# GpSimd writes a buffer of its own behind each gather, and waits for it once per pair

## The chip, the cores and the metric

One core of one Trainium2 chip runs the kernel. The metric is the device time of the whole launch in microseconds (us); here it is the median of several executions. The engines are called PE (TensorE), DVE (VectorE), ACT (ScalarE), POOL (GpSimd) and SP (SyncE). The trace also splits off PEld, the weight loads of TensorE.

## The reference, cut to what matters

A graph of 12,500 nodes with 128 features and 212,500 edges, sorted by their target node, goes through three rounds of message passing. Two use one of eight weight matrices per edge type, the third is a plain graph convolution.

```python
def _rgcn_layer(x, W, SW, b, src, dst, rel):          # twice, W is [8, 128, 128]
    xt = jnp.einsum('nd,rde->rne', x, W)
    msg = xt[rel, src]
    agg = jax.ops.segment_sum(msg, dst, num_segments=x.shape[0])
    return jax.nn.relu(agg + x @ SW + b)
...
x = _layernorm(x + _L0_gnn_ref(...))                   # two layers of the above
feat = jax.nn.relu(x @ W1 + b1)
h = feat * d_invsqrt
agg = jax.ops.segment_sum(h[src], dst, num_segments=N)
feat = feat - agg * d_invsqrt
x = _layernorm(x + feat @ W2 + b2)
```

## The kernel before, in words

**Tiles, groups, pairs, iterations.** The edges are cut into tiles of 128. Seven tiles (`KG`) are a group, two groups a pair (`PAIR`, so `PT` = 14 tiles), four pairs an iteration (`UN` = 56 tiles). A pass over the edges has 29 full iterations and a rest of three pairs, 119 pairs in all (`NGP`). There are three passes: r1 reads the input `x`, r2 reads `x1_d` (the result of r1, `x_d` in the trace), r3 reads `h_d`. r1 and r2 come from `relational_sum`, r3 from `plain_sum`, and all three get their rows from `Gathers`.

**The gathers.** For each tile POOL issues one indirect DMA (line 781) that fetches the 128 rows of the tile's source nodes into one of the 56 slots of `c.rows`. The indices lie in `c.idx`, which ACT copies into place one pair at a time (`take`, `put`, line 735). Each gather adds 16 to the semaphore `landed` of its group as its data arrives. Ahead of a pair POOL waits for two things: `idx_ready` (the indices are there) and `summed` (PE has finished the pair that stood in the same 14 slots one iteration, that is 56 tiles, earlier). So POOL can be at most four pairs ahead of PE. The first 14 tiles of r2 and 21 of r3 are fetched by `early` (line 761) while the pass before still ends.

**What takes the rows.** PE waits for a group's `landed`, multiplies each tile with a one-hot matrix `S` that DVE builds (line 1023 in r1 and r2, line 1216 in r3), and adds into a PSUM bank (line 961 in r1 and r2, line 1186 in r3); its last matmul of a group (in r3 of a pair) adds 1 to `summed`. In r1 and r2 ACT then copies the bank to `agg` (line 885), and once an iteration PE multiplies `agg` with the eight weight matrices (line 931) and DVE adds the outcome to `acc` (line 1062). In r3 DVE adds the bank to `acc` itself (line 1243). DVE's `one_hot` for the pair after next waits for `summed` of this pair. The node-wise work of a finished chunk (`Tail1` to `Tail3`, transposes such as line 1343) is placed between the pairs.

**Order.** Nothing schedules at run time: each engine runs its own instruction stream in the order of the code, and the streams meet at semaphores alone. POOL's stream in the passes is nothing but gathers, register arithmetic and the waits at a pair's start. `gate` adds 1 to a semaphore that nobody waits for.

Of the kernel before, what the change touches and what calls it, by code (L numbers as in the profile page):

```python
# [12 lines left out]
P = 128  # L13
# [12 lines left out]
PR = RING // PAIR  # L26
PT = PAIR * KG
# [10 lines left out]
class Part:  # L38


    def __init__(self, at, tiles):
        self.at, self.tiles, self.groups = at, tiles, len(tiles)
        self.pairs = range(at, at + len(tiles) // PAIR)
# [9 lines left out]
NGP = NG // PAIR  # L53
# [53 lines left out]
def gate(eng, passed):  # L107

    eng.sem_inc(passed, 1)
# [7 lines left out]
def build(nc, x, src, dst, rel, w1, sl1, b1, w2, sl2, b2, gw1, gb1, gw2, gb2, out):  # L117
    with ExitStack() as top:
        def sb(name, shape, dt=F32):
            return top.enter_context(nc.sbuf_tensor(name, shape, dt))  # L120
# [9 lines left out]
        c = Shared()  # L130
# [20 lines left out]
        c.gs_i = sb("gs_i", [1, RING + NG], I32)  # L151
        c.gs8 = sb("gs8", [1, NG])
        c.step_t, c.step_g, c.carry = sb("step_t", [P, 1]), sb("step_g", [P, 1]), sb("carry", [P, 1])
        c.found = sb("found", [NODES, DEG_COLS + COLS])
        c.deg = sb("deg", [DEG_ROWS, DEG_PARTS, NODES])
        c.dinv = sb("dinv", [P, NB])
# [524 lines left out]
def rounds_of(eng, c, which, most):  # L681
    return eng.value_load(c.rounds_i[0:1, which:which + 1], min_val=1, max_val=most)


def halves(part, h):


    tiles = part.of(h)
    return (tiles + 1) // 2 if part is not FULL and h >= (ENDS - 1) * PAIR else tiles


class Gathers:
# [3 lines left out]
    def __init__(self, nc, top, c, tag, table, which, turns, incs, then):  # L696
        def sem(name):
            return top.enter_context(nc.semaphore(f"{tag}_{name}"))

        self.c, self.table, self.which, self.incs = c, table, which, incs  # L700
        self.most = N // GN + 2 if which else 4 * (N // GN + 1) + 1
        self.turns, self.then = turns, then
        self.landed = [sem(f"landed{h}") for h in range(RING + PAIR)]
        assert [s.num - self.landed[0].num for s in self.landed] == list(range(RING + PAIR))
        self.cleared = sem("cleared")
        self.idx_ready = sem("idx_ready")
        self.summed = sem("summed")

# [57 lines left out]
    def run(self, pool, ready, stored):  # L766

        def iteration(q, i, part, set_of, skip=0):
            at = set_of * UN
            for p in part.pairs:  # L770
                if (p + 1) * PT <= skip:
                    continue
                pool.wait_ge(self.idx_ready, (q * (IT + 1) + i) * PR + p + 1)
                pool.wait_ge(self.summed, self.pairs_summed(q, i, p))
                gate(pool, self.c.passed)
                for h in range(p * PAIR, (p + 1) * PAIR):
                    for k in range(part.of(h)):
                        s, slot = h * KG + k, h if k < halves(part, h) else RING + h % PAIR
                        if s < skip:
                            continue  # L780
                        pool.indirect_dma_start(  # L781
                            out=self.c.rows[:, self.place(s), :], out_offset=None, in_=self.table[:, :],
                            in_offset=bass.IndirectOffsetOnAxis(ap=self.c.idx[:, at + s:at + s + 1], axis=0)
                        ).then_inc(self.landed[slot], 16)

        def one_round(q, skip=0):
            iteration(q, 0, FULL, 0, skip)
            with pool.Fori(0, IT // SETS) as n:
                i = pool.snap(n * SETS)
                iteration(q, i + 1, FULL, 1)  # L790
                iteration(q, i + 2, FULL, 0)
            iteration(q, IT, LEFT, 1)

        self.begin(pool)
        pool.sem_inc(self.cleared, 1)
        one_round(0, EARLY[self.turns])
        if ready is not None:
            pool.wait_ge(ready, 1)
            gate(pool, self.c.passed)
        rounds = rounds_of(pool, self.c, self.which, self.most)  # L800
        with pool.If(rounds > 1):
            with pool.Fori(1, rounds) as q:
                pool.wait_ge(self.summed, q * (self.incs * NGP) + self.incs * PR)
                gate(pool, self.c.passed)

                landed = range(self.landed[0].num, self.landed[0].num + len(self.landed))
                pool.dma_reset(landed)
                pool.sem_clear(landed)
                pool.sem_inc(self.cleared, 1)
                one_round(q)  # L810
        pool.end_ifs()
        if self.then is not None:
            self.early(pool, rounds, stored)

# [539 lines left out]
class Sets:  # L1354
# [14 lines left out]
    def sb(self, name, shape):  # L1369
        return self.ctx.enter_context(self.nc.sbuf_tensor(f"{self.tag}_{name}", shape, F32))  # L1370

    def sem(self, name):
        return self.c.top.enter_context(self.nc.semaphore(f"{self.tag}_{name}"))
# [413 lines left out]
```

## Time and profile before

| | before |
|---|---|
| time, median of 3 runs | 7520.16 us (7511.46 to 7523.07) |
| the profiled execution | 7492.37 us, of which the span of the core is 7490.5 us |
| POOL busy | 4709.2 us (63%), 4992 instructions |
| PE busy | 3400.0 us (45%) |
| DVE, ACT busy | 1713.6 us (23%), 399.8 us (5%) |
| DMA | 382.84 MB, 51 GB/s over the span |
| gathers of line 781 | 1661 in r1, 1647 in r2, 1640 in r3, together 4948 |

The profile lists for each instruction when it started and how long it was busy, and for each idle stretch ahead of one what ended it. "issue" is idle time that ended by nothing the profile can name, "remote" or "an unknown queue" one that ended by a semaphore whose sender the profile could not name. Busy shares are means over the whole span.

### The profile page before, as it was taken

To read this page: it belongs to the slowest core of one execution; us is meant where nothing else is said; L and a number is where in the kernel's file an instruction comes from. 1 tells how busy PE (TensorE), PEld (TensorE's weight loads), DVE (VectorE), ACT (ScalarE), POOL (GpSimd) and SP (SyncE) were. 2 spreads that over 40 slices of the span, in tenths; PEclk is the share of its full clock that TensorE was granted. 3 is DMA by queue.
4 is the path that set the end of the run, shared out by engine and by line. 5 is a ranking of instruction groups with operands and counts; after the bars stand their busy time and mean duration, and the time that the engine had idled before them with its cause. 6 is when DMAs were issued, how large, how long until landed. Compare 5 with 4: busy or idle time off the path is not lost.

```text
span 7490.5 us, 50657 instructions
## 1 busy us (share of the span) xinstructions
PE 3400.0 (45%) x13687; PEld 2488.9 (33%) x13841; DVE 1713.6 (23%) x2844; ACT 399.8 (5%) x915; POOL 4709.2 (63%) x4992
## 2 busy tenths in 40 slices
PE   2455455445545454455545544554333333333333
PEld 1333333333333333333333333334333333333333
DVE  3333333333333212222212121221111111111111
ACT  1000000000000000000000000000000000000000
POOL 5666666666666456666666666645666666666665
PEclk7666676666667677767777776775555555555555
DMA  2111111111111111112211211211111111111111
GB/s 57 46 51 49 50 52 50 50 48 51 50 50 53 39 42 54 54 54 57 56 54 55 58 54 56 56 44 44 52 50 51 50 53 51 53 48 52 52 51 48
DMA packets 197581, 382.84 MB, mean 51 GB/s; under 512 B 84323, under 2 KB 93327, under 8 KB 197543
## 3 DMA queue, kind: packets, MB, share of 16 engines
q0 software_dynamic: 159456, 326.88, 16.7%
q1 hardware_dynamic: 36416, 54.67, 2.1%
q10 hardware_dynamic: 1670, 0.85, 0.0%
q8 instruction: 15, 0.25, 0.0%
q14 instruction: 24, 0.19, 0.0%
HBM read 356.43 MB, written 25.65 MB: 51 GB/s over the span
## 4 chain that ended last, share of the span: by engine, by line
another core or an unknown queue 51%; issue 25%; PE 16%; DVE 5%; DVEq 1%; ACT 1%; ACTq 0%; DMA 0%; SPq 0%
PE bank L931 5%; PE bank L961 4%; PE bank L1186 4%; DVE r_S L1023 1%; DVE r_hot L1018 1%; ACT r_agg L885 1%; DVE acc L1062 0%; PE bank L1576 0%; PE bank L945 0%; PE bank L1572 0%; PE bank L1707 0%; DVE d_st L1750 0%; DVEq L1052 0%; DVE d_zr L1762 0%
## 5 line engine op out<-in xcount | busy, mean ns | idle before, releaser
L781 POOL DMA_INDIRECT rows<-in_x_dram,idx x1661 | 1567.6, 944 | 917.3 <-issue 511.9
L781 POOL DMA_INDIRECT rows<-x_d,idx x1647 | 1555.1, 944 | 885.0 <-issue 503.9
L781 POOL DMA_INDIRECT rows<-h_d,idx x1640 | 1552.4, 947 | 825.3 <-issue 790.4
L961 PE MATMUL bank<-r_S,rows 128*128 128x128 f32 x6644 | 1205.3, 346 | 519.5 <-issue 402.4
L1186 PE MATMUL bank<-r_S,rows 128*128 128x64 f32 x3322 | 772.5, 386 | 1425.1 <-issue 1386.9
L961 PEld LDWEIGHTS bank<-r_S,rows 128*128 128x128 f32 x6644 | 1149.5, 258 | 362.3 <-issue 337.5
L1186 PEld LDWEIGHTS bank<-r_S,rows 128*128 128x128 f32 x3322 | 759.4, 317 | 1440.7 <-issue 1440.3
L1023 DVE TENSOR_TENSOR r_S<-bank,key 128x1792 f32<-128x1792 f32 x238 | 480.4, 2019 | 917.3 <-remote 815.8
L885 ACT COPY r_agg<-bank 128x512 f32<-128x512 f32 x476 | 265.8, 586 | 4400.9 <-remote 3081.1
L945 PEld LDWEIGHTS bank<-zeros_bf 128*128 128x128 bf16 x476 | 55.9, 117 | 1267.7 <-ACT r_agg L885 892.3
L1243 DVE TENSOR_TENSOR acc<-acc,bank 128x64 f32 x238 | 52.7, 222 | 1833.1 <-remote 1658.4
L931 PE MATMUL bank<-r_agg,w1s 128*128 128x512 f32 (+1 forms) x528 | 458.1, 1036 | 5.5 <-issue 4.0
L931 PE MATMUL bank<-r_agg,w2s 128*128 128x512 f32 (+1 forms) x528 | 457.5, 1034 | 2.3 <-ACT r_agg L885 2.3
L1018 DVE TENSOR_TENSOR r_hot<-bank,b_spot 128x1344 bf16<-128x1344 f32 x119 | 185.4, 1558 | 1010.0 <-remote 980.4
L945 PE MATMUL bank<-zeros_bf 128*128 128x512 bf16 x323 | 166.5, 515 | 473.7 <-ACT r_agg L885 386.1
L1021 DVE TENSOR_REDUCE r_placed<-r_hot 128x192 bf16<-128x1344 bf16 x119 | 290.4, 2441 | 4.1
L954 PE MATMUL bank<-one_bf,r_placed 128*32 128x1 bf16 x714 | 36.9, 167 | 479.8 <-ACT r_agg L885 300.3
L1062 DVE TENSOR_TENSOR acc<-acc,bank 128x64 f32 x492 | 109.2, 222 | 626.7 <-issue 230.3
L1572 PE MATMUL bank<-ident,d_fT 128*109 128x128 f32 (+2 forms) x114 | 33.3, 445 | 467.0 <-DVE d_fT L1647 448.5
L931 PEld LDWEIGHTS bank<-r_agg,w1s 128*128 128x128 f32 x528 | 114.5, 220 | 314.6 <-issue 314.0
L931 PEld LDWEIGHTS bank<-r_agg,w2s 128*128 128x128 f32 x528 | 110.1, 209 | 312.1 <-issue 311.1
L1572 PEld LDWEIGHTS bank<-ident,d_fT 128*109 128x109 f32 (+2 forms) x114 | 24.0, 285 | 474.6 <-DVE d_fT L1647 455.8
(151 smaller groups left out, 1545.6 us busy)
## 6 DMA issues: line engine op xcount, KB each, us to landing
rows<-in_x_dram,idx POOLq DMA_INDIRECT x1661
rows<-x_d,idx POOLq DMA_INDIRECT x1647
rows<-h_d,idx POOLq DMA_INDIRECT x1640
d_xr<-in_x_dram SPq DMA_DIRECT2D x54, 218.0 KB
x_d<-d_yr SPq DMA_DIRECT2D x27, 218.0 KB
d_x1r<-x_d SPq DMA_DIRECT2D x27, 218.0 KB
h_d<-d_hr SPq DMA_DIRECT2D x27, 218.0 KB
part_d<-d_pr SPq DMA_DIRECT2D x27, 218.0 KB
```

The source lines that it names most:

```text
L781: pool.indirect_dma_start(out=self.c.rows[:, self.place(s), :], out_offset=None, in_=self.table[:, :], in_offset=bass.IndirectOffsetOnAxis ...
L885: act.copy(agg[:, h, :, :], agg_ps[h % BUFS][:, :].rearrange("p (n r) -> p n r", r=NREL)).then_inc(agg_out, 1)
L931: mm = pe.matmul(mix_ps[:, 0:groups * GN], W[:, r, :], agg[:, first:first + groups, :, r], start=(r == 0), stop=(r == NREL - 1))
L945: pe.matmul(agg_ps[j][:, :], c.zeros_bf[:, :], c.zeros, start=True, stop=False, skip_group_check=True)
L961: mm = pe.matmul(agg_ps[j][:, bass.ds(offs[j * KG + k], TK)], c.rows[:, g.place(h * KG + k), :], S[:, pb, j * KG + k, :], start=False, sto ...
L1018: ch.then(dve.tensor_tensor(hot[:, b, :, :], spots.unsqueeze(1).broadcast_to([P, PT, SPOTS]), bc_last(blocks.spot[:, at], SPOTS), ALU.is_e ...
L1021: dve.tensor_reduce(placed[:, b, :, :], hot[:, b, :, :].rearrange("p (j k) n -> p j n k", k=KG), AX.X, ALU.add)
L1023: dve.tensor_tensor(S[:, b, :, :], c.iota[:, :].unsqueeze(1).broadcast_to([P, PT, TK]), bc_last(c.key[:, at], TK), ALU.is_equal).then_inc( ...
L1062: ins = dve.tensor_tensor(window, window, mix_ps[:, w * GN:(w + 1) * GN], ALU.add)
L1186: mm = pe.matmul(sum_ps[b][:, j * GN:(j + 1) * GN], c.rows[:, g.place(h * KG + k), :], S[:, b, j * KG + k, :], start=(k == 0), stop=(k == ...
L1243: ins = dve.tensor_tensor(window, window, sum_ps[p % BUFS][:, j * GN:(j + 1) * GN], ALU.add)
L1572: mm = pe.transpose(self.PH[ch.s][0:ch.p, a * P:(a + 1) * P], self.fT[ch.s][:, a * ch.p:(a + 1) * ch.p], c.ident[:, :])
```

## The change

A buffer `pause` with 14 slots of 128x128 float32 is added, and a semaphore `paused` for each pass. Behind each gather of line 781 POOL now zeroes one slot of that buffer; nothing reads it. The write behind the last gather of a pair adds 1 to `paused`, and ahead of each pair POOL waits, besides the waits it had, until the last such write of the pair before is done. At a pass's end it waits once more. Pairs that are skipped because `early` fetched them add their 1 at once. The gathers of `early` (line 761 before) get no write.

```diff
+        c.pause = sb("pause", [P, PT, P])
...
+        self.paused = sem("paused")
...
             for p in part.pairs:
                 if (p + 1) * PT <= skip:
+                    pool.sem_inc(self.paused, 1)
                     continue
                 pool.wait_ge(self.idx_ready, (q * (IT + 1) + i) * PR + p + 1)
                 pool.wait_ge(self.summed, self.pairs_summed(q, i, p))
+                pool.wait_ge(self.paused, q * NGP + i * PR + p + 1)
                 gate(pool, self.c.passed)
                 for h in range(p * PAIR, (p + 1) * PAIR):
                     for k in range(part.of(h)):
...
                             in_offset=bass.IndirectOffsetOnAxis(ap=self.c.idx[:, at + s:at + s + 1], axis=0)
                         ).then_inc(self.landed[slot], 16)
+                        ins = pool.memset(self.c.pause[:, s % PT, :], 0.0)
+                ins.then_inc(self.paused, 1)
...
         self.begin(pool)
         pool.sem_inc(self.cleared, 1)
+        pool.sem_inc(self.paused, 1)
         one_round(0, EARLY[self.turns])
...
         pool.end_ifs()
+        pool.wait_ge(self.paused, rounds * NGP + 1)
+        gate(pool, self.c.passed)
         if self.then is not None:
             self.early(pool, rounds, stored)
```

On POOL, at the border of two pairs in the loop of r1, the order before was this (a count stands for gathers in a row, in brackets the semaphores that the first of a pair waits for):

```order
L781 DMA rows<-in_x_dram,idx 128x128 x13
L773 REGISTER_ALU
L774 REGISTER_ALU [waits r1_idx_ready]
L781 DMA rows<-in_x_dram,idx 128x128 [waits r1_summed]
L781 DMA rows<-in_x_dram,idx 128x128 x13
```

At the same place of the changed kernel, where the gather is line 785 and the write line 789, POOL has:

```order
L785 DMA rows<-in_x_dram,idx 128x128
L789 MEMSET pause 128x128
L776 REGISTER_ALU
L777 REGISTER_ALU [waits r1_idx_ready]
L785 DMA rows<-in_x_dram,idx 128x128 [waits r1_summed,r1_paused]
L789 MEMSET pause 128x128
L785 DMA rows<-in_x_dram,idx 128x128
```

The row of 14 gathers has become 14 gathers and 14 writes in turn, and the first gather of a pair has a second wait. The streams of PE, DVE, ACT and SP are what they were.

## Rows read from the trace of the kernel before

**Rows 1.** The profile's page: span, engine shares, chain that ended last.
```profile
span 7490.5 us, 50657 instructions
...
PE 3400.0 (45%) x13687; PEld 2488.9 (33%) x13841; DVE 1713.6 (23%) x2844; ACT 399.8 (5%) x915; POOL 4709.2 (63%) x4992
...
another core or an unknown queue 51%; issue 25%; PE 16%; DVE 5%; DVEq 1%; ACT 1%; ACTq 0%; DMA 0%; SPq 0%
```

**Rows 2.** Groups of POOL's instructions: busy us, mean ns, idle before and releasers.
```profile
L781 POOL DMA_INDIRECT rows<-in_x_dram,idx x1661 | 1567.6, 944 | 917.3 <-issue 511.9 <-remote 289.5 <-PE bank L961 113.2
L781 POOL DMA_INDIRECT rows<-x_d,idx x1647 | 1555.1, 944 | 885.0 <-issue 503.9 <-remote 310.1 <-PE bank L961 62.7
L781 POOL DMA_INDIRECT rows<-h_d,idx x1640 | 1552.4, 947 | 825.3 <-issue 790.4 <-ACT idx L735 34.6 <-remote 0.3
...
L401 POOL MEMSET ident<- 128x128 f32 x1 | 0.2, 204 | 0.3 <-POOLq L1777 0.3
```

**Rows 3.** POOL's timeline in r2: start, duration, instruction, idle before.
```profile
3015.78 0.94 POOL L781 DMA_INDIRECT rows<-x_d,idx  x1 [0.30 <-issue]
3017.02 0.94 POOL L781 DMA_INDIRECT rows<-x_d,idx  x1 [0.30 <-issue]
```

**Rows 4.** POOL's waits: total us, times, longest.
```profile
POOL rows L781 <- issue: 1806.3, 4802, 11.1
POOL rows L781 <- remote: 600.0, 125, 6.2
POOL rows L781 <- PE bank L961: 175.8, 18, 53.0
```

**Rows 5.** Timeline of all engines around a stop of POOL in r2.
```profile
3201.80 0.94 POOL L781 DMA_INDIRECT rows<-x_d,idx  x1 [5.71 <-remote]
...
3228.51 2.76 PE L961 MATMUL bank<-r_S,rows 128*128 128x128 f32 x14
...
3231.10 0.96 PE L1343 MATMUL bank<-ident,d_pre 128*109 128x128 f32 x4
...
3235.51 0.94 POOL L781 DMA_INDIRECT rows<-x_d,idx  x1 [0.30 <-issue]
3241.55 1.07 ACT L885 COPY r_agg<-bank 128x512 f32<-128x512 f32 x2 [16.46 <-remote]
3241.81 2.02 DVE L1023 TENSOR_TENSOR r_S<-bank,key 128x1792 f32<-128x1792 f32 x1 [14.18 <-remote]
...
3242.47 0.94 POOL L781 DMA_INDIRECT rows<-x_d,idx  x1 [6.01 <-remote]
...
3244.68 0.94 POOL L781 DMA_INDIRECT rows<-x_d,idx  x1 [1.27 <-issue]
```

**Rows 6.** Timeline of all engines around a stop of POOL in r3.
```profile
6164.15 0.95 POOL L781 DMA_INDIRECT rows<-h_d,idx  x1 [0.30 <-issue]
...
6167.44 0.27 PE L1186 MATMUL bank<-r_S,rows 128*128 128x64 f32 x1 [1.85 <-issue]
...
6171.63 1.97 PE L1186 MATMUL bank<-r_S,rows 128*128 128x64 f32 x8 [0.23 <-issue]
6171.84 0.57 DVE L1243 TENSOR_TENSOR acc<-acc,bank 128x64 f32 x2 [32.91 <-remote]
...
6172.50 0.94 POOL L781 DMA_INDIRECT rows<-h_d,idx  x1 [7.40 <-issue]
```

**Rows 7.** POOL's timeline at the start: memsets ahead of the first gather.
```profile
0.26 0.10 POOL L1777 MEMSET const-float32-0.0<- 128x1 f32 x1 [0.26 <-issue]
0.29 0.10 POOL L1777 MEMSET const-float32-1.0<- 128x1 f32 x1
...
0.75 0.20 POOL L401 MEMSET ident<- 128x128 f32 x1 [0.29 <-POOLq L1777]
```

**Rows 8.** Line 781 alone in the stretches of r1, r2 and r3.
```profile
0.00:2485.00 2485.00, 1566.15 (x1660) 0.69 0.19 50
2562.00:4999.00 2437.00, 1554.12 (x1646) 0.72 0.20 54
5065.00:7470.00 2405.00, 1552.38 (x1640) 0.51 0.19 51
```

## The prediction

> **What bounds the kernel now.** I read the page first. POOL is busy for 63% of the span, more than any other engine, and half of the chain that ended last is credited to a sender that the profile can't name [rows 1]. On a kernel whose rows all arrive by indirect DMA that sender could be either the gathers landing or something that holds a semaphore back. The busy share does not settle it, so I went to POOL's own groups: 4948 gathers of line 781, 944 to 947 ns each, with 2627.6 us of idle time ahead of them [rows 2]. The timeline shows what that idle time is made of. Gathers stand 1.24 to 1.25 us apart, 0.94 busy and 0.30 idle, and this goes on across pair borders too [rows 3]. So 4948 x 1.248 = 6175 us of the 7490.5 are POOL at its steady pace, which is the floor of the kernel as it stands. The 0.30 us gaps are 4948 x 0.304 = 1504 us of the idle time; the other 2627.6 - 1504 = 1123 us are real stops. The rest, some 190 us, is the start, the two borders between passes and the last chunk. By pass the line's busy time is 1566, 1554 and 1552 us of 2485, 2437 and 2405 us [rows 8]: the three passes behave alike, and nothing but POOL takes nearly their whole length.
>
> The stops are at pair borders, in the row "remote" 125 times, 600.0 us, and at PE's bank 18 times, 175.8 us [rows 4]; in r3 they are hidden under "issue". There, 825.3 - 1640 x 0.304 = 327 us at 7.1 us a stop (7.40 less the usual 0.30) are some 45 stops. That makes about 190 in all, against 355 pairs that POOL issues.
>
> What a stop waits for is `summed`, but what makes `summed` late is strange. In r2 PE's matmuls of a pair start at 3228.51 and a transposition that follows them at 3231.10. POOL issues its last gather at 3235.51 and has to stop. ACT, DVE and POOL, which all wait for that pair, go on only at 3241.55, 3241.81 and 3242.47, some 5.1 us after the last gather ended and 10 us after PE seems done [rows 5]. In r3 PE advances one matmul in 2.1 us while gathers run, still at 6167.44, and eight at once from 6171.63, again after POOL has stood still for more than 5 us (its last gather ended at 6165.10) [rows 6]. So PE, or its signals, are slow while POOL gathers and recover about 5 us after it stops. PE is no bound by its own work (45% busy), but together with the four-pair ring it makes POOL stop.
>
> **What the change costs, part by part.** *The write behind a gather.* POOL's chain is serial and is the floor, so whatever the write adds counts 4948 times. No row shows a memset behind a gather. The nearest are at the start: four 128x1 memsets start 0.03 us apart though each is shown as 0.10 long, and the 128x128 one, of just the size that the change writes, as 0.20 [rows 7], 204 ns [rows 2]. Short instructions overlap, so the fixed 0.10 is latency and 0.03 occupancy; the 127 more columns are 0.20 - 0.10 = 0.10 us. I take 0.03 + 0.11 = 0.14 us. From below it could be nothing, if the write fits in the 0.30 us between two gathers; from above it is 0.20 + 0.30 = 0.50, its shown length and a second gap. I keep 0.14 since memsets in a row show no gap, and a gather's 1.25 us pace held for 28 and more in a row looks like an engine at its limit rather than a feeder's. 4948 x 0.14 = +693 us.
>
> The Trainium skill, page "Perfetto Trace Analysis", section "GPSIMD Engine Instruction", warns that a GpSimd duration in a profile is unreliable and that start-to-start spacing should be used. By the shown 204 ns the term would be 4948 x 0.204 = 1009 us and the sum 8.50 ms; by spacing it is the sum below. This case's four memsets (0.03 apart, 0.10 long) agree with the page.
>
> *The wait at a pair's start.* Today the first gather of a pair follows the last of the pair before by 0.30 us. With a wait on POOL's own last write it can't be made ready ahead. From the release of a waiting POOL to its gather rows 5 show 3242.47 - 3241.81 = 0.66 to 3242.47 - 3241.55 = 0.92 us; less the 0.30 that is there anyway this is 0.36 to 0.62, and I take 0.5. At the 190 borders where POOL stops for `summed` in any case it costs nothing, at the other 355 - 190 = 165 it does: +83 us. If the stops went away it would be 355 x 0.5 = +178. Behind the wait stand only the next pair's gathers; PE waits for those in turn, and it has up to four pairs in hand.
>
> *What the slower pace gives back.* 28 gathers take 28 x 0.14 = 3.9 us longer between two stops, and in that time PE gets somewhat further. But the release was tied to POOL standing still, not to the time since the last stop, and a break of 1.27 us in the stream ended nothing (3244.68, then gathers as before) [rows 5]. So I let only a tenth of the 1123 us go: -110 us.
>
> *The rest.* The wait and increment at a pass's end are three times below 1 us, behind gathers that `early` follows; the two borders already hold waits of tens of us. The write traffic is in SBUF, so DMA is untouched. DVE's operations don't wait for POOL's writes, unless by a shared port: DVE is busy 23% of the time, and were each write delayed by half of a DVE instruction it met, it would be inside the bound above.
>
> Sum: 7492.4 + 693 + 83 - 110 = 8158 us for the profiled execution. The median of the runs is 27.8 us above the profiled one, so 8186; I say **8185 us**.
>
> **The rivals.**
>
> *(b) The write is hidden in the gap.* If the 0.30 us between gathers are idle also for the cores that write, only the waits cost: 7520 + 83, about 7600 us. For it speaks that the gap is longer than the 0.20 of the write; against it that the gap has the same length in nearly every row, as if it were part of the gather. The Trainium skill's page "GPSIMD Engine Reference", section "4. When to use GPSIMD", says that two of the eight cores make a gather's descriptors; by section "2.1 Instruction dispatch" each core begins the next instruction when its own share is done. Six cores would then write for nothing but the two would still add their share, and no row here separates cores. I give (b) 0.12.
>
> *(c) The slower pace relieves PE: faster.* The stops exist because something between POOL's gathers and PE's completions falls behind. If it works off a backlog at a fixed rate, the pace of POOL decides. Stops and recoveries put that rate near the mean pace of a cycle: the two resumptions at 3201.80 and 3242.47 are 40.7 us apart with (3235.51 - 3201.80)/1.248 + 1 = 28 gathers between them [rows 5], 1.45 us each, and the new pace would be 1.248 + 0.14 + 0.5/14 = 1.42 us. At that pace the stops could shrink to little. Of the 1123 us about 1000 are such stops (the longest, 53.0 us [rows 4], and the 34.6 us of r3 [rows 2] belong to the starts of passes). Then 7520 + 693 + 178 - 1000 = 7391 us. It decides for faster as long as a write adds less than (1000 - 178)/4948 = 0.166 us. Against it: a write is one more instruction on the engine whose activity seems to disturb, and short breaks have cured nothing so far. I give it 0.27, of which 0.21 end faster, 0.02 within 0.2%, 0.04 slower.
>
> *(d) The write costs far more than its row,* with a gap of its own, up to 0.50 us: 4948 x 0.50 = 2474, thus near 10 ms. Above 8.7 ms I put 0.05.
>
> *(e) Nothing changes,* because the writes run beside all else and the waits are over when they are reached: 7520 us, 0.03.
>
> **How the numbers follow.** The main case has 0.53 and its own range of 7900 to 8700 us (0.07 to 0.25 us per write, and none to a third of the stops given back). Rivals (b) and (e) lie between 7500 and 7700, (c) between 7200 and 7600. The range must reach (c) to hold 8 in 10: from 7350 to 8700 about 0.08 stays out below and 0.06 above. For this kernel 0.2% is 15 us, about what its runs can tell. Faster has the 0.21 of (c); within 0.2% lie 0.02 of (c) and the 0.03 of (e); slower has the rest, 0.74.
>
> **What the changed profile would show.** The step for the write is right if the spacing of gathers within a pair is 1.39 us; 1.25 means (b), 1.7 (d). The step for the wait is right if the gap ahead of a pair's first gather without a stop is 0.8 us. The step for the stops is right if POOL still stops every 28 gathers in r1 and r2 for 5 to 6 us, and 7 us in r3, and if ACT and DVE still start together 5 us after POOL's last gather. If the line's real stops are far below 1123 us, (c) holds and the sum is wrong by that term; PE's matmuls would then run at 0.1 to 0.2 us steps while POOL gathers. The prediction is most easily wrong there, since it rests on breaks of about 1 us and no row shows a slower steady pace.

## The result, and the profile after

| | before | after |
|---|---|---|
| median | 7515.81 us (7492.89 to 7523.07, 4 runs) | 7328.76 us (7325.21 to 7331.44, 4 runs) |
| profiled span | 7490.5 us | 7329.4 us |

The ratio is 0.9756, 95% interval [0.9734, 0.9778]: the changed kernel is 2.4% faster. The forecast was 8185 us, in a range of 7350 to 8700. It had the wrong sign, and its range missed by 21 us. Rival (c), "the slower pace relieves PE", had said 7391 us.

The page of the kernel after, the rows that answer to [rows 1]:

```profile
span 7329.4 us, 55900 instructions
...
PE 3589.1 (49%) x13840; PEld 2539.2 (35%) x13841; DVE 1719.9 (23%) x2844; ACT 405.5 (6%) x915; POOL 5855.1 (80%) x9940
...
another core or an unknown queue 44%; issue 23%; PE 16%; POOL 8%; DVE 5%; DVEq 1%; ACT 1%; ACTq 1%; DMA 0%; SPq 0%; POOLq 0%
```

POOL is busy 1146 us longer and the span is 161 us shorter. The chain has much the same make-up as before, with 8% for POOL. Next, the groups of POOL's instructions after (the gather is line 785 now, the write line 789), which answer to [rows 2]:

```profile
L785 POOL DMA_INDIRECT rows<-in_x_dram,idx x1661 | 1588.3, 956 | 467.4 <-issue 337.4 <-remote 109.0 <-PE bank L970 15.6
L785 POOL DMA_INDIRECT rows<-x_d,idx x1647 | 1575.5, 957 | 453.1 <-issue 339.3 <-remote 90.2 <-PE bank L970 13.4
L785 POOL DMA_INDIRECT rows<-h_d,idx x1640 | 1567.3, 956 | 422.4 <-issue 357.8 <-ACT idx L737 43.2 <-POOL pause L789 10.5
L789 POOL MEMSET pause<- 128x128 f32 x4948 | 1100.5, 222 | 3.9 <-issue 0.2
```

The idle time ahead of the gathers is 467.4 + 453.1 + 422.4 = 1342.9 us, where it was 2627.6. Its kinds are seen on POOL's timeline in r2 of the kernel after, at the same moment as [rows 5]:

```profile
3200.10 0.95 POOL L785 DMA_INDIRECT rows<-x_d,idx  x1 [0.17 <-issue]
3201.05 0.23 POOL L789 MEMSET pause<- 128x128 f32 x1
3204.33 0.95 POOL L785 DMA_INDIRECT rows<-x_d,idx  x1 [3.06 <-remote]
3205.29 0.22 POOL L789 MEMSET pause<- 128x128 f32 x1
3205.67 0.95 POOL L785 DMA_INDIRECT rows<-x_d,idx  x1 [0.17 <-issue]
...
3224.24 0.95 POOL L785 DMA_INDIRECT rows<-x_d,idx  x1 [0.80 <-issue]
```

Within a pair, gathers start 5.67 - 4.33 = 1.34 us apart: 0.95 for the gather, 0.22 for the write and 0.17 idle. It was 1.25 [rows 3], so a write adds 0.09 us and not the 0.22 that it is shown to last. The 0.30 us gap has shrunk to 0.17, so part of the write lies in it. A pair that PE doesn't hold up starts after 0.80 us, which is 0.63 more than the gap between a write and a gather inside a pair. A stop is now 3.06 us here, where it was 5.71 and 6.01.

POOL's waits after, the answer to [rows 4]:

```profile
POOL rows L785 <- issue: 1034.5, 4842, 2.0
POOL rows L785 <- remote: 206.5, 71, 3.7
...
POOL rows L785 <- PE bank L970: 29.0, 6, 9.8
```

Waits for a sender without a name fell from 125 to 71 and from 600.0 to 206.5 us, those for PE's bank from 18 to 6 and from 175.8 to 29.0 us, and the longest under "issue" from 11.1 to 2.0 us. Line 785 alone, in the stretches of r1, r2 and r3 (answers to [rows 8]), shows that the clock and the DMA share have not moved, so neither explains the gain:

```profile
0.00:2410.00 2410.00, 1579.49 (x1652) 0.69 0.19 52
2490.00:4850.00 2360.00, 1558.69 (x1630) 0.71 0.20 56
4910.00:7290.00 2380.00, 1554.10 (x1627) 0.51 0.19 51
```

What moved is PE. All engines' timeline in r3 of the kernel after, at the time of [rows 6]:

```profile
6169.75 0.26 PE L1195 MATMUL bank<-r_S,rows 128*128 128x64 f32 x1 [0.43 <-issue]
...
6173.93 0.95 POOL L785 DMA_INDIRECT rows<-h_d,idx  x1 [0.17 <-issue]
6174.81 0.58 DVE L1252 TENSOR_TENSOR acc<-acc,bank 128x64 f32 x2 [39.45 <-remote]
...
6175.27 0.95 POOL L785 DMA_INDIRECT rows<-h_d,idx  x1 [0.17 <-issue]
...
6181.03 0.27 PE L1195 MATMUL bank<-r_S,rows 128*128 128x64 f32 x1 [1.83 <-issue]
...
6184.55 0.26 PE L1195 MATMUL bank<-r_S,rows 128*128 128x64 f32 x1 [1.14 <-issue]
6185.96 0.26 PE L1195 MATMUL bank<-r_S,rows 128*128 128x64 f32 x1 [1.15 <-issue]
6187.36 0.27 PE L1195 MATMUL bank<-r_S,rows 128*128 128x64 f32 x1 [1.14 <-issue]
```

In this stretch PE is still far slower than its work asks (0.27 us of work in each 1.40), but before it took 2.1 us for the same step [rows 6]. Steps of 2.1 us have become rarer and are not gone (6181.03 above). And DVE, which waits for PE, was released at 6174.81 while gathers went on at 1.34 us; in [rows 6] the release came 6.7 us after POOL's last gather had ended (6171.84 and 6165.10). Counted over r3, DVE's additions to `acc` that had waited over 1 us began in the midst of gathers in 48 of 91 cases before and in 93 of 111 after.

### The profile page after: what moved, and what is told of

Same layout as the page of the kernel before. It is cut to its first block, busy times and chain, and to the rows that moved or that the text cites. A ratio compares the mean times of both kernels' runs of the same rounds, so it can differ in the third digit from the quotient of the medians.

```text
span 7329.4 us, 55900 instructions
## 1 busy us (share of the span) xinstructions
PE 3589.1 (49%) x13840; PEld 2539.2 (35%) x13841; DVE 1719.9 (23%) x2844; ACT 405.5 (6%) x915; POOL 5855.1 (80%) x9940
## 4 chain that ended last, share of the span: by engine, by line
another core or an unknown queue 44%; issue 23%; PE 16%; POOL 8%; DVE 5%; DVEq 1%; ACT 1%; ACTq 1%; DMA 0%; SPq 0%; POOLq 0%
POOL rows L785 6%; PE bank L970 6%; PE bank L940 5%; PE bank L1195 2%; POOL pause L789 1%; DVE r_S L1032 1%; PE bank L954 1%; DVE r_hot L1027 1%; DVE acc L1071 1%; ACT r_agg L894 0%; DVEq L1061 0%; PE bank L1574 0%; PE bank L1430 0%; PE bank L1560 0%
## 5 line engine op out<-in xcount | busy, mean ns | idle before, releaser
L785 POOL DMA_INDIRECT rows<-in_x_dram,idx x1661 | 1588.3, 956 | 467.4 <-issue 337.4
L785 POOL DMA_INDIRECT rows<-x_d,idx x1647 | 1575.5, 957 | 453.1 <-issue 339.3
L785 POOL DMA_INDIRECT rows<-h_d,idx x1640 | 1567.3, 956 | 422.4 <-issue 357.8
L1195 PE MATMUL bank<-r_S,rows 128*128 128x64 f32 x3322 | 804.6, 397 | 1398.0 <-issue 760.3
L970 PE MATMUL bank<-r_S,rows 128*128 128x128 f32 x6644 | 1296.2, 355 | 336.3 <-issue 333.0
L970 PEld LDWEIGHTS bank<-r_S,rows 128*128 128x128 f32 x6644 | 1196.3, 264 | 419.6 <-issue 398.2
L1195 PEld LDWEIGHTS bank<-r_S,rows 128*128 128x128 f32 x3322 | 760.2, 318 | 1442.8 <-issue 1047.0
L789 POOL MEMSET pause<- 128x128 f32 x4948 | 1100.5, 222 | 3.9 <-issue 0.2
L954 PE MATMUL bank<-zeros_bf 128*128 128x512 bf16 x476 | 244.4, 514 | 1364.6 <-issue 732.8
L940 PEld LDWEIGHTS bank<-r_agg,w2s 128*128 128x128 f32 x528 | 125.5, 239 | 332.3 <-issue 331.0
L1225 DVE TENSOR_TENSOR r_S<-bank,key 128x896 f32<-128x896 f32 x119 | 129.8, 1092 | 35.9 <-DVE acc L1252 18.8
L737 ACT COPY idx<-src_i x360 | 71.3, 203 | 1101.7 <-remote 729.0
```

The costliest lines, as they stand in the source:

```text
L785: pool.indirect_dma_start(out=self.c.rows[:, self.place(s), :], out_offset=None, in_=self.table[:, :], in_offset=bass.IndirectOffsetOnAxis ...
L789: ins = pool.memset(self.c.pause[:, s % PT, :], 0.0)
L940: mm = pe.matmul(mix_ps[:, 0:groups * GN], W[:, r, :], agg[:, first:first + groups, :, r], start=(r == 0), stop=(r == NREL - 1))
L954: pe.matmul(agg_ps[j][:, :], c.zeros_bf[:, :], c.zeros, start=True, stop=False, skip_group_check=True)
L970: mm = pe.matmul(agg_ps[j][:, bass.ds(offs[j * KG + k], TK)], c.rows[:, g.place(h * KG + k), :], S[:, pb, j * KG + k, :], start=False, sto ...
L1195: mm = pe.matmul(sum_ps[b][:, j * GN:(j + 1) * GN], c.rows[:, g.place(h * KG + k), :], S[:, b, j * KG + k, :], start=(k == 0), stop=(k == ...
```

## The experiments

Eighteen runs were made, on six chips of two kinds, and the chip turned out to matter more than any edit. The kernel before took 7506.47, 7476.58 and 7510.84 us on chips 6, 1 and 15, much as in the result above; I call these *chips with stops*. It took 6281.45, 6286.93 and 6280.06 us on chips 9, 3 and 13, *chips without stops*. Each chip was measured in one sitting only, so "chip" here stands for all that stayed the same in that sitting. Ratios are always to the kernel before on the same chip.

All diffs below are against the changed kernel, unless they say otherwise.

### The parts of the change, on chip 6

**One write per pair, and the wait** (e1).

```diff
                         ).then_inc(self.landed[slot], 16)
-                        ins = pool.memset(self.c.pause[:, s % PT, :], 0.0)
+                ins = pool.memset(self.c.pause[:, 0, :], 0.0)
                 ins.then_inc(self.paused, 1)
```

> One write per pair (behind its last gather) and the wait for it at the next pair, no writes behind the other 13 gathers. Theory P (pace: PE is relieved because a gather now comes every 1.34 us instead of 1.25): the pace inside a pair is 1.25 us again, so the stops come back nearly in full (about 1000 us), the waits add some 80 us, and the time is 7550 to 7620 us. Rival W (wait: relief comes from POOL's queue running empty once per pair, 0.8 us): the stops stay as low as with the whole change (about 275 us), the pace saves 4948 x 0.09 = 445 us, and the time is near 6900 us.

Measured: 7506.93 us, ratio 1.0005 [0.9993, 1.0016]. POOL's timeline of this kernel in r2:

```profile
3312.50 0.94 POOL L785 DMA_INDIRECT rows<-x_d,idx  x1 [0.30 <-issue]
3313.43 0.23 POOL L789 MEMSET pause<- 128x128 f32 x1
3318.88 0.95 POOL L785 DMA_INDIRECT rows<-x_d,idx  x1 [5.22 <-remote]
3320.13 0.95 POOL L785 DMA_INDIRECT rows<-x_d,idx  x1 [0.31 <-issue]
...
3336.09 0.22 POOL L789 MEMSET pause<- 128x128 f32 x1
3337.11 0.95 POOL L785 DMA_INDIRECT rows<-x_d,idx  x1 [0.80 <-issue]
```

The time is a little below the 7550 expected, and the waits for a sender without a name are as many as before (132, 603.0 us). The wait alone gains nothing, and it also costs nothing. A pair that doesn't stop is 0.22 + 0.80 - 0.30 = 0.72 us longer, up to 355 x 0.72 = 256 us over the kernel, and the time is unchanged. POOL's added time has only taken the place of stops.

**All the writes, with the wait one pair late** (e2): the buffer has twice the slots in bf16, and the wait is for the write before the last.

```diff
-        c.pause = sb("pause", [P, PT, P])
+        c.pause = sb("pause", [P, 2 * PT, P], BF16)
...
-        pool.sem_inc(self.paused, 1)
+        pool.sem_inc(self.paused, 2)
```

> All 4948 writes stay (of 128 bf16 elements instead of 128 float32, so that twice the slots fit), but the wait is for the write of the pair before last, which is always long done, so POOL's queue never runs empty. Theory P: stops stay low, some 275 us plus what the gaps at pair starts had covered, and the 0.63 us per pair (220 us) go: 7150 to 7250 us. Rival W: the stops come back (about 1000 us): 7329 - 220 + 700 = 7800 us.

Measured: 7535.68 us, 1.0043 [1.0031, 1.0056]. The pace is 1.33 to 1.34 us, so 4948 x 0.09 = 445 us were added to POOL for +29 us of time. Neither expectation came out (7150 to 7250, and 7800). Without the break at a pair's start the slower pace cancels itself but wins nothing, and PE's idle time under "issue" in r3 is 1385.7 us, as in the kernel before (1386.9).

**Writes of 128x1, and the wait** (e3).

```diff
-                        ins = pool.memset(self.c.pause[:, s % PT, :], 0.0)
+                        ins = pool.memset(self.c.pause[:, s % PT, 0:1], 0.0)
```

> Each write is 128x1 instead of 128x128; the wait stays. It takes about 0.1 us less of POOL's time, so the pace of gathers falls back to 1.25 to 1.28 us. Theory P: with the pace back the stops come back by most of 1000 us, time 7500 to 7700 us. Rival K (kind: what relieves PE is that another kind of instruction stands between two gathers, whatever its length): stops stay near 275 us and the time is 6900 to 7100 us.

Measured: 7496.6 us, 0.9989 [0.9977, 1.0001], no difference that can be told. The small write is shown as 117 ns long, and the pace stays 1.25 us: it lies wholly in the gap. So 4948 additional instructions on POOL do nothing by themselves.

**Fourteen writes behind the last gather of a pair, none between** (e4).

```diff
                         ).then_inc(self.landed[slot], 16)
-                        ins = pool.memset(self.c.pause[:, s % PT, :], 0.0)
+                for t in range(PT):
+                    ins = pool.memset(self.c.pause[:, t, :], 0.0)
                 ins.then_inc(self.paused, 1)
```

> The same number of writes, but all 14 of a pair behind its last gather instead of one behind each; the wait stays. Theory P in its simple form (mean pace over tens of us counts): the mean pace is that of the whole change or a little slower (14 x 0.14 us of writes + 0.6 us wait per pair), stops stay low, 7350 to 7500 us. Rival K and a local form of P (the spacing between two gathers counts): the gathers are 1.25 us apart inside a pair and the stops come back: 6175 + 119 x 3 x 2.6 + 190 + 700 to 1000, about 8000 us.

Measured: 7369.8 us, 0.9821 [0.98, 0.9842], within what was expected if the mean pace counts. POOL's timeline of this kernel in r2, then one of its waits and PE's group in r3:

```profile
3201.64 0.94 POOL L785 DMA_INDIRECT rows<-x_d,idx  x1 [0.30 <-issue]
3202.59 2.12 POOL L790 MEMSET pause<- 128x128 f32 x14
3205.55 0.95 POOL L785 DMA_INDIRECT rows<-x_d,idx  x1 [0.84 <-issue]
3206.80 0.94 POOL L785 DMA_INDIRECT rows<-x_d,idx  x1 [0.30 <-issue]
```

```profile
POOL rows L785 <- remote: 8.4, 7, 1.7
```

```profile
L1196 PE MATMUL bank<-r_S,rows 128*128 128x64 f32 x3322 | 767.4, 424 | 1550.1 <-DMA rows<-h_d,idx 1481.3 <-issue 61.1 <-DVE r_S L1226 7.7
```

The pace in a pair is the old 1.25 us, and yet the waits for a sender without a name have gone from 600.0 to 8.4 us, and PE's idle time under "issue" in r3 from 1386.9 to 61.1 us. Each pair carries one break of 2.12 + 0.84 = 2.96 us, 2.66 more than the usual gap, 355 x 2.66 = 944 us in all. That alone on the 6281 us of a chip without stops would be about 7225 us, so some 145 us of short waits seem to be left. So the slower pace is not needed: a regular break relieves PE too, if it is near 3 us. This also speaks against my reading of [rows 5], by which only a stop of 5 us helped.

### Chip 9, where there was nothing to gain

The next four were to settle the size of the break and the source of PE's slowness, and met a chip where the kernel before takes 6281.45 us.

**Seven writes at the pair's end** (e5, as e4 with `range(KG)`).

> Seven writes, not 14, behind the last gather of each pair, and the wait. Theory R (PE's speed depends on how densely POOL gathers over some tens of us, POOL stops when PE falls behind, and added POOL time up to a point only takes the place of stops): a pair's added time is about 7 x 0.137 + 0.6 = 1.6 us, between wait-only (0.5 us, stops as before) and 14 at the end (2.8 us, no stops). 355 x 1.6 = 570 us are added to 6175 + 205, and the stops left are 200 to 500 us: 7150 to 7450 us, faster than both ends if relief sets in early. Rival T (the time is the mean of the ends, relief grows in a straight line): 7440 us.

Measured: 6910.85 us, 1.1002 [1.0984, 1.102]; the 7150 to 7450 were expected for a chip with stops.

**Two writes behind each gather** (e8), of bf16 like e2's, with the wait as in the change.

```diff
-                        ins = pool.memset(self.c.pause[:, s % PT, :], 0.0)
+                        for w in range(2):
+                            ins = pool.memset(self.c.pause[:, 2 * (s % PT) + w, :], 0.0)
```

> Two writes (128 bf16 elements each) behind each gather, wait kept. The pace becomes 1.48 us. Theory R: no stops are left to save beyond the 275 us of the change, so POOL's own time rules: 4948 x 1.48 + 355 x 0.6 + 205 = 7740 us, slower than before. Rival K (each instruction between gathers relieves PE further): stops zero and the same 7740 us, so this run tells only whether the last 275 us go: 7740 without, 8000 with them.

Measured: 7688.57 us, 1.2241 [1.222, 1.2261]. The pace is 1.48 us: the second write adds 0.14 where the first added 0.09.

**No gathers at all** (e6), against the kernel before: POOL fills each slot by a write, in `early` too, and the reset of the gathers' semaphores goes.

```diff
-                        pool.indirect_dma_start(
-                            out=self.c.rows[:, self.place(s), :], out_offset=None, in_=self.table[:, :],
-                            in_offset=bass.IndirectOffsetOnAxis(ap=self.c.idx[:, at + s:at + s + 1], axis=0)
-                        ).then_inc(self.landed[slot], 16)
+                        ins = pool.memset(self.c.rows[:, self.place(s), :], 0.0)
+                        ins.then_inc(self.landed[slot], 16)
...
-                pool.dma_reset(landed)
```

> POOL writes zeros into the row slots instead of gathering them (in the passes and ahead of them), everything else is kept; so all node rows of the messages are left out. It shows how fast PE, ACT and DVE are without gathers. Theory R: PE then runs at its own speed, 3400 to 3600 us of busy time plus its waits in the node-wise parts, 4000 to 5000 us in all, and no matmuls stand on steps of 0.7 us. Rival S (PE is slow by its own doing, whatever POOL does): steps of 0.7 us stay and the time stays above 6500 us.

Measured: 3197.55 us (one run), below the 4000 to 5000 expected.

**Gathers of a quarter of a row** (e7), against the kernel before. The other three quarters of each slot are zeroed once at the start.

```diff
-                            out=self.c.rows[:, self.place(s), :], out_offset=None, in_=self.table[:, :],
+                            out=self.c.rows[:, self.place(s), 0:32], out_offset=None, in_=self.table.rearrange("n (a d) -> (n a) d", a=4)[:, :],
```

> The kernel before (no writes, no added wait), but each gather brings 32 of the 128 columns, so three quarters of the gathered data are left out and the number of gathers and of their rows stays. If it is the issuing of gathers by POOL that slows PE (theory R with POOL as the source), the pace stays 1.25 us, the stops stay near 1000 us and the time near 7500 us. If it is the arriving data (rival D, traffic into SBUF or from HBM), the stops go with most of the bytes: 6400 to 6700 us.

Measured: 6291.4 us (one run), pace 1.25 us. A gather has the same price for a quarter of the bytes.

### Chip 1: the two kinds of chip told apart

> The changed kernel as it is. On the chip of the second set the kernel before took 6281 us, not 7507: it had no stops. Theory C (PE's slowness while POOL gathers is a property of the chip, and the change only trades POOL time against it): where the kernel before takes about 6280 us, the changed one has nothing to win and takes 6281 + 4948 x 0.09 + 355 x 0.63 = 6950 us (ratio 1.107); where it takes about 7510 us, the changed one takes 7329 again (ratio 0.976). Rival: the second set's chip was quick for another reason and the change's ratio is the same 0.976 there, 6130 us.

e9, the changed kernel: 7395.33 us against 7476.58, 0.9902 [0.9872, 0.9931]. It is faster here too, by less than in the result and than the 0.976 expected (its waits for a sender without a name are 90 times 278.0 us, against 71 times 206.5).

> The kernel before, for its profile on this call's chip. If the time is about 6280 us, theory C expects the pace of 1.25 us without stops and no matmuls on steps of 0.7 us; if it is about 7510 us, the profile of the kernel before as shown, 1000 us of stops.

e10, the kernel before with a profile: 7482.22 us (one run), with 909.6 + 885.9 + 823.8 = 2619.3 us idle ahead of the gathers, as in [rows 2].

> Seven writes behind each pair's last gather, and the wait. Where the kernel before takes about 6280 us: 6911 again. Where it takes about 7510 us, theory R expects 7150 to 7450 us (6175 + 205 + 570 of added time and 200 to 500 of stops), less than the 7370 of 14 writes at the end if relief sets in early.

e11, seven writes at the pair's end, as e5: 7450.68 us, 0.9969 [0.9959, 0.9979], at the upper end of what was expected; PE's idle time under "issue" in r3 is still 1222.0 us. The same edit cost 629 us on chip 9 (6910.85 - 6281.45) and gained 26 us here.

> No gathers in the passes (all message rows left out, POOL writes zeros into the row slots). It took 3198 us on the chip of the second set. Theory R with gathers as the cause: 3198 us also where the kernel before takes 7510. Rival S (PE of that chip is slow by itself): far longer there, above 4000 us, with matmuls on steps of 0.7 us.

e12, without gathers, as e6: 3234.84 us (one run). The engine shares on its page, then its group of PE's matmuls in r3, then the same group of the kernel before (from the trace of the result; e10's has 1403.3 us under "issue"):

```profile
PE 2788.5 (86%) x13687; PEld 1986.2 (61%) x13841; DVE 1706.3 (53%) x2844; ACT 404.8 (13%) x915; POOL 769.7 (24%) x4992
```

```profile
L1182 PE MATMUL bank<-r_S,rows 128*128 128x64 f32 x3322 | 611.5, 375 | 25.7 <-DVE r_S L1212 25.2 <-issue 0.5
```

```profile
L1186 PE MATMUL bank<-r_S,rows 128*128 128x64 f32 x3322 | 772.5, 386 | 1425.1 <-issue 1386.9 <-DVE r_S L1216 37.9
```

Chips 1 and 9 agree to 1.2% once no gather runs (3235 and 3198), and differ by 19% with them (7477 and 6281). PE's idle time for no named reason in r3, 1386.9 us before, is 0.5 us without gathers. So the slowness of PE belongs to the gathers, and only to some chips.

### Chip 3: the change where there are no stops

**The changed kernel** (e15).

> The changed kernel once more. My theory (the change adds about 0.09 us to each of 4948 gathers and 0.63 us at each of 355 pair starts, 670 us in all, and takes stops away only where there are some): on a chip with stops 0.975 to 0.99, pace 1.34 us; on a chip where the kernel before takes about 6281 us and has none, about 6950 us, 1.09 to 1.11. Rival (the writes speed something up besides the stops): below 1.0 on either kind of chip.

Measured: 7002.42 us against 6286.93, ratio 1.114 [1.1122, 1.1159]: the change that gains 2.4% in the result costs 11.4% here. Its gathers and its PE group in r3:

```profile
L785 POOL DMA_INDIRECT rows<-in_x_dram,idx x1661 | 1584.3, 954 | 373.2 <-issue 365.2 <-POOL pause L789 5.4 <-DVE idx L496 2.6
L785 POOL DMA_INDIRECT rows<-x_d,idx x1647 | 1570.6, 954 | 367.8 <-issue 363.3 <-POOL pause L789 4.5
L785 POOL DMA_INDIRECT rows<-h_d,idx x1640 | 1565.0, 954 | 379.7 <-issue 275.9 <-POOL pause L789 103.8
```

```profile
L1195 PE MATMUL bank<-r_S,rows 128*128 128x64 f32 x3322 | 768.0, 424 | 1479.1 <-DMA rows<-h_d,idx 1473.0 <-DVE r_S L1225 6.1
```

No wait for a sender without a name is left, and PE's idle time ends by rows landing: PE keeps up, and POOL is the bound.

**Quarter rows once more** (e13), and the groups of its gathers:

> The kernel before with gathers that fetch only the first 32 of a row's 128 columns (the other 96 of each slot stay zero, so three quarters of the gathered data are left out): as many gathers, as many descriptors, a quarter of the bytes. Two theories for what slows PE while POOL gathers. By the number of gathers: the time is that of the kernel before within 0.5% on this chip, the pace 1.25 us, and on a chip with stops there are as many as before (about 1050 us of them). By the bytes: the stops are gone, and the time is the floor, about 6280 us, 0.84 of before on a chip with stops. On a chip without stops both give about 6290 us and it tells nothing.

```profile
L784 POOL DMA_INDIRECT rows<-in_x_dram,idx x1661 | 1574.2, 948 | 507.0 <-issue 504.8 <-DVE idx L497 1.3 <-PE bank L964 0.9
L784 POOL DMA_INDIRECT rows<-h_d,idx x1640 | 1558.8, 950 | 499.6 <-issue 499.3 <-ACT idx L738 0.3
L784 POOL DMA_INDIRECT rows<-x_d,idx x1647 | 1557.8, 946 | 501.8 <-issue 501.8
```

Measured: 6288.53 us, 1.0004 [0.9994, 1.0013]. It moves as the kernel before does, so its idle time of 507.0 + 499.6 + 501.8 = 1508.4 us stands for that of the kernel before without stops; for the changed kernel it is e15's 373.2 + 367.8 + 379.7 = 1120.7 us. With these two, the stops in the result can be read off by difference: 2627.6 - 1508.4 = 1119 us before, 1342.9 - 1120.7 = 222 us after.

**Ten writes at the pair's end** (e14, as e4 with `range(10)`) and **two writes behind each gather** (e16, as e8).

> Ten writes of 128x128 behind the last gather of each pair and the wait, none behind the other gathers. My theory (PE catches up while POOL doesn't gather, and needs some 3 us more per pair than the steady pace leaves it): the block lasts about 10 x 0.2 + 0.6 = 2.6 us, 355 x 2.6 = 923 us in place of stops; on a chip with stops a result between the seven (0.997) and the fourteen (0.982), near 0.985 to 0.99. If only the full stop that ends by itself counts (rival: a pause below some length gives nothing), it is as the seven or worse, 0.997 to 1.01. On a chip without stops 6281 + 923 = 7200 us, 1.14 to 1.15.

> Two writes behind each gather and the wait per pair. On the chip without stops this had a pace of 1.48 us and took 7689 us. My theory (POOL's own time is then the whole kernel, stops or none): 7690 to 7760 us on any chip, stops below 60 us in all, thus about 1.025 on a chip with stops. Rival (stops come on top of POOL's time in any case): a chip with stops adds at least 275 us, the least that the changed kernel kept: 7960 us or more.

Measured: 7056.53 us, 1.1227 [1.1209, 1.1246], below the 7200 expected (the ten writes and the wait add 770 us and not 923), and 7690.2 us, 1.2233 [1.2213, 1.2254], 2 us from e8. Neither could tell anything about stops on a chip that has none.

### Number or bytes: chips 13 and 15

The quarter-row kernel was run twice more, to meet a chip with stops.

> The gathers of a quarter of each row once more (three quarters of the gathered data left out). On a chip where the kernel before takes about 7500 us: by the number of gathers, a time within 0.5% of before with as many stops; by the bytes, about 6290 us, 0.84. On a chip where before takes about 6285 us: 6290 us by both.

> The gathers of a quarter of each row a fourth time (three quarters of the gathered data left out). On a chip where the kernel before takes about 7500 us: by the number of gathers, a time within 0.5% of before with as many stops; by the bytes, about 6290 us, 0.84. On a chip where before takes about 6285 us: 6290 us by both.

e17 (chip 13, before 6280.06): 6291.75 us, 1.0019 [1.0008, 1.0031]. e18 (chip 15, before 7510.84): 7514.9 us, 1.0 [0.9985, 1.0015]. The gathers and PE's timeline in r3 of e18:

```profile
L784 POOL DMA_INDIRECT rows<-in_x_dram,idx x1661 | 1568.9, 945 | 969.0 <-issue 500.6 <-PE bank L964 254.1 <-remote 213.0
L784 POOL DMA_INDIRECT rows<-x_d,idx x1647 | 1556.1, 945 | 857.9 <-issue 498.7 <-remote 298.9 <-PE bank L964 52.1
L784 POOL DMA_INDIRECT rows<-h_d,idx x1640 | 1553.7, 947 | 813.9 <-issue 779.4 <-ACT idx L738 34.5
```

```profile
6184.02 0.26 PE L1189 MATMUL bank<-r_S,rows 128*128 128x64 f32 x1 [2.54 <-issue]
6186.82 0.27 PE L1189 MATMUL bank<-r_S,rows 128*128 128x64 f32 x1 [2.53 <-issue]
6188.92 0.27 PE L1189 MATMUL bank<-r_S,rows 128*128 128x64 f32 x1 [1.84 <-issue]
```

With a quarter of the bytes the idle time is 2640.8 us, as much as the 2627.6 of [rows 2], and PE takes 2.1 to 2.8 us a matmul. So it is not the bytes. What is left is the number of gathers, or of the pieces they are cut into; that number was not varied by itself.

## Why the prediction was wrong

**The floor and the stops** were right. The steady pace of 1.248 us gives 6175 us, and chips without stops take 6280 to 6287 us. The stops were put at 1123 us; by the difference above they are 1119.

**The write** was put at 0.14 us from the memsets at the start, and measured 0.09: +445 us in place of +693. **The wait** was put at 0.5 us, and measured 0.63. The sign named for it, a gap of 0.8 us ahead of a pair's first gather, came out. With the stops mostly gone it counts at nearly each pair, 355 x 0.63 = 224 us in place of 83. The two make 669 us. Where nothing else moves, on chip 3, the change cost 7002.42 - 6286.93 = 715 us; some 46 us of that lie in neither term. 776 was forecast for them. That they missed by little together is partly luck, since the write was 248 us too high and the wait 141 too low.

**The step that failed is "What the slower pace gives back".** It let a tenth of the stops go, 110 us. They fell from 1119 to 222 us, by 897. With the 715 for POOL's own time, taken over from chip 3, that makes -182 us, where the profiled spans differ by -161. Two thoughts carried the step, and both fell:

- *"The release was tied to POOL standing still."* This took one stop in r2 and one in r3 for the rule. In r3 of the kernel before, PE also ran at full speed with gathers at 1.25 us around it, and turned slow some 15 us after POOL had gone on:

```profile
6112.57 0.94 POOL L781 DMA_INDIRECT rows<-h_d,idx  x1 [7.56 <-issue]
...
6121.30 0.94 POOL L781 DMA_INDIRECT rows<-h_d,idx  x1 [0.31 <-issue]
6121.75 6.07 PE L1186 MATMUL bank<-r_S,rows 128*128 128x64 f32 x28
...
6129.60 0.27 PE L1186 MATMUL bank<-r_S,rows 128*128 128x64 f32 x1 [1.79 <-issue]
...
6135.23 0.26 PE L1186 MATMUL bank<-r_S,rows 128*128 128x64 f32 x1 [2.53 <-issue]
```

  Counted over r3 of that trace, in the first 15 us after a stop 2200 of 2287 matmuls of line 1186 followed the one before within 0.6 us, and between 15 and 60 us 197 of 888. So a stop buys PE a spell at full speed, and the question is how long a break has to be, and how often it has to come. With a write behind each gather and a break per pair (after), the slow steps are mostly 1.4 us and fewer are 2.1 to 2.8, and DVE is released in the midst of gathers (6174.81 after). With a break of 2.96 us after each 14 gathers, some 17 us, PE hardly turns slow at all (61.1 us in e4).
- *"A break of 1.27 us in the stream ended nothing."* e1 confirms this: with its 0.8 us breaks the time is that of before. But I took from it that a slower pace would do as little. Neither half of the change gains by itself on chip 6 (e1 +0.05%, e2 +0.43%); the two together do elsewhere (-2.4% in the result, -1.0% on chip 1). The whole change was not run on chip 6, so that it takes both is likely and not shown on one chip.

**Beneath this lies a wrong addition.** I held POOL's pace to be the floor "so whatever the write adds counts 4948 times", and set the give-back against it as a small correction. On a chip with stops the loop of POOL and PE is set by how fast PE works off pairs; what POOL gains it loses again in the next stop. POOL's time per gather, with writes and all idle time ahead of both, is 1.48 us before, 1.48 in e1, 1.49 in e2, 1.48 in e3 and 1.45 after. The same shows in four edits that add time to POOL and move the end by half a per cent at most: e1 (up to 256 us added, +0.05%), e2 (445 us, +0.43%), e3 (-0.11%), and e11 (629 us by its twin e5, -0.31%). A price in POOL's time was due in full only where POOL is the bound, as on chips 9 and 3.

**Rival (c)** had the direction and, in the main, the mechanism: the stops shrank because PE fell behind less. Its point of decision held, since a write adds 0.09, below 0.166 us. But it laid this to the pace, and e2 has the pace without the gain and e4 the gain without the pace. By mean time per gather it fares better: e4's is 1.25 + 2.66/14 = 1.44 us, near the 1.45 that it named. Nor did its sign come out, matmuls in steps of 0.1 to 0.2 us while POOL gathers: in r3 after, steps of 1.4 us are common. It said +693 + 178 = 871 of cost and 1000 of relief; measured were 715 and 897. Both were too high, and in the sum the errors cancelled in part: -129 us against -182. The evidence I had against it was a short break that cured nothing, and one such break says little of a slower pace with a break in every pair. (b) fell, since the pace rose, though 0.13 of the 0.22 us are hidden; (d) and (e) fell.

**Open.** Why the same change gives 2.4% in the result and 1.0% on chip 1. What makes a chip one with stops, and whether a chip stays so from one sitting to another. Whether 14 writes at the pair's end beat one behind each gather: they were not run on one chip (0.9821 on chip 6; 0.9902 on chip 1). Whether two writes per gather would clear all stops on a chip that has them. How long a break must be: 0.8 us (e1) does nothing, 2.96 us (e4) nearly all. And what it is on PE's side that waits: the profile names no sender.

## What to carry to other kernels

Where two engines hold each other up through a ring, don't add a cost to the pace of the one that stops: first ask which of them sets the length of the cycle, for instance with a run that adds a known time to one and nothing else; if the end doesn't move, that time was free. Idle time on a compute engine that ends by nothing named, and goes away when the gathers are taken out, is a toll of the gathers, and shrinking each gather to a quarter did not lower it; what did was a break of 3 us after every 14. Whether fewer gathers would is not shown. And before keeping a change that buys relief with an engine's own time, measure it on several chips: this one is worth -2.4%, -1.0% or +11.4%.

## What the runs showed of the hardware that was not expected

- **Chips differ by 19 to 20% on one kernel.** Six chips gave 6280.06, 6281.45, 6286.93 and 7476.58, 7506.47, 7510.84 us, with nothing between. Without gathers two of them, one of each kind, gave 3197.55 and 3234.84 us.
- **Dense indirect gathers slow PE on some chips.** At one gather of 128 rows in 1.25 us, matmuls of 0.27 us started 2.1 and 2.8 us apart (e18); at one in 1.34 us with a break of 0.8 us per pair, often 1.40 us apart (after). A quarter of the bytes changed nothing (1.0 [0.9985, 1.0015]).
- **The slowness sets in late.** After a stop of POOL (7.56 us at 6112.57 before), PE ran at full speed beside gathers for some 15 us and was slow from 6129.60 on. A break of 2.96 us after every 14 gathers left 61.1 us of PE's unnamed idle time in r3 (e4), against 1386.9.
- **A POOL write is hidden in part behind a gather.** One of 128x1, shown as 117 ns, adds nothing; one of 128x128, shown as 222 ns, adds 0.09 us; a second one adds 0.14 us (1.48 - 1.34, both of bf16 in e8).
